# New written orders for every engine, half of the weight transfers on ACT's queue, and a reshaped finish

## The reference: what is computed

```python
for i in range(3):                       # three SSM layers, 64 states
    dbc   = x @ W_dbc[i].T               # delta (1), B (64), C (64)
    delta = softplus(delta @ W_dt[i].T + b_dt[i])
    h_t   = exp(delta * -exp(A_log)) * h_(t-1) + delta * x * B
    x     = (h * C).sum(states) + D * x
    if i < 2: x = mean of neighbouring pairs of steps     # 375 -> 187 -> 93
h = x + attention(layernorm(x))          # 8 heads of 8, Taylor form of softmax
out = h + moe(layernorm(h))              # router, softmax, top 2 of 6 experts, 3-layer MLP each
```

## Time and profile before

| | us |
|---|---|
| median of 3 runs | 836.59 |
| lowest, highest | 832.17, 836.82 |
| the profiled execution: its time | 834.02 |
| the profiled execution: span, first to last instruction | 832.1 |
| PE busy, DVE busy, ACT busy, POOL busy | 708.4, 635.7, 532.2, 330.6 |
| one turn of the steady middle | 44.6 |
| mean granted TensorE clock | 0.953 of full speed |

### The profile page before, as it was taken

One profiled execution on the slowest core, in us unless ns is written; L12 is line 12 of the kernel. 1 busy time (PEld: TensorE's weight loads), 2 busy tenths in 40 slices (PEclk: granted clock), 3 DMA queues, 4 the chain that ended last, 5 costly groups with the idle time before them and its releaser, 6 DMA issues.

```text
span 832.1 us, 18813 instructions
## 1 busy us (share of the span) xinstructions
PE 708.4 (85%) x7751; PEld 318.6 (38%) x7751; DVE 635.7 (76%) x1079; ACT 532.2 (64%) x930; POOL 330.6 (40%) x287
## 2 busy tenths in 40 slices
PE   4665689799989999898989898989989898988773
PEld 2322334244444444443434443444434333433321
DVE  5777869698988888888988888898768895645330
ACT  2334376769686877868686858686766848484630
POOL 4454552325263545354453525263433434121000
PEclk9878899899999999999999999999989999999975
DMA  3223211102021111202030312120110100000001
GB/s 71 55 52 83 47 46 34 33 11 54 19 49 32 45 36 29 52 20 61 8 72 3 69 30 51 31 51 11 44 37 2 34 10 16 15 2 10 7 5 23
DMA packets 78562, 28.30 MB, mean 34 GB/s; under 512 B 70276, under 2 KB 78468, under 8 KB 78468
## 3 DMA queue, kind: packets, MB, share of 16 engines
q1 hardware_dynamic: 75268, 26.43, 14.0%
q10 hardware_dynamic: 3200, 0.58, 0.4%
HBM read 13.28 MB, written 3.05 MB: 20 GB/s over the span
## 4 chain that ended last, share of the span: by engine, by line
PE 57%; DVE 15%; ACT 8%; SPq 7%; DMA 4%; issue 4%; POOL 3%; POOLq 0%; DVEq 0%; ACTq 0%
PE ring L970 16%; PE ring L1038 5%; SPq L554 4%; PE ring L1125 4%; PE ring L1097 4%; PE ring L1026 3%; PE ring L1002 3%; PE ring L1106 3%; PE ring L1062 2%; PE ring L943 2%; PE ring L1088 2%; ACT pm L834 2%; ACT hid L869 2%; PE ring L1054 2%; PE ring L977 1%
## 5 line engine op out<-in xcount | busy, mean ns | idle before, releaser
L834 ACT ACTIVATE pm<-ring,two_col 93x744 f32<-93x744 f32 x128 | 105.2, 871 | 12.8 <-PE ring L1026 11.9
L1402 DVE TENSOR_TENSOR hidw<-hid,ring 128x744 f32<-128x744 f32 x48 | 44.5, 928 | 43.3 <-PE ring L1088 32.4
L690 POOL TENSOR_TENSOR h_in<-base_D,carry_D 128x372 f32<-128x372 f32 x16 | 15.6, 977 | 138.3 <-DVE base_D L1288 112.2
L1038 PE MATMUL ring<-pm,v 97*32 97x93 f32 x2048 | 55.6, 251 | 11.9 <-ACT pm L834 9.0
L770 ACT ACTIVATE soft_A<-ring,bdt_col 128x744 f32<-128x744 f32 x16 | 14.1, 880 | 80.6 <-PE ring L970 80.6
L869 ACT ACTIVATE hid<-ring,b_col 128x372 f32<-128x372 f32 x96 | 49.3, 566 | 23.5 <-PE ring L1106 23.3
L1026 PE MATMUL ring<-q_exp,qk 32*93 32x372 f32 x512 | 57.6, 520 | 7.8 <-POOL q_exp L708 2.6
L1106 PE MATMUL ring<-nrm_f,w 64*64 64x372 f32 x384 | 41.6, 505 | 22.1 <-DVE quad_D L1272 13.0
L686 POOL TENSOR_TENSOR du_C<-delta_C,x_C 128x744 f32<-128x744 f32 x16 | 29.5, 1841 | 75.8 <-ACT delta_C L782 55.6
L693 POOL TENSOR_TENSOR base_C<-base_C,carry_C 128x744 f32<-128x744 f32 x16 | 40.1, 2507 | 48.2 <-DVE base_C L1288 27.0
L1038 PEld LDWEIGHTS ring<-pm,v 97*32 97x32 f32 x2048 | 42.3, 112 | 41.0 <-ACT pm L834 21.7
(11 more groups left out here) (277 smaller groups left out, 1862.2 us busy)
## 6 DMA issues: line engine op xcount, KB each, us to landing
xin_A<-in_x_dram SPq DMA_DIRECT2D x62, 93.0 KB
xin_B<-in_x_dram SPq DMA_DIRECT2D x62, 93.0 KB
x_A<-x_A SPq DMA_DIRECT2D x32, 93.0 KB, 2.2
x_B<-x_B SPq DMA_DIRECT2D x32, 93.0 KB, 2.6
x_C<-x_C SPq DMA_DIRECT2D x32, 93.0 KB, 2.2
out_dram<-osb SPq DMA_DIRECT2D x16, 186.0 KB
x_D<-x_D SPq DMA_DIRECT2D x32, 46.5 KB, 2.0
w<-in_L_ffn_expert_w_dram SPq DMA_DIRECT2D x10, 48.0 KB
```

What stands on the lines that cost most here:

```text
L834: a.activation(pm[q % 2][h][0:TOUT].rearrange("m a j n -> m a (j n)"), out_of(f"att.s{q}{h}")[0:TOUT, :, 0:COLS], ACT.Square, bias=two_col ...
L1038: ins = mm(o[32 * j:32 * j + 32, 0, at:at + TOUT], v1[:, q, H * h + 4 * b + j, :], pm[q % 2][h][:, b, j, :], start=True, stop=True, tile_p ...
L1402: tt(hidw[k][:], hid2[:], out_of(f"ffn.g_{k}")[:, :, 0:COLS], ALU.mult).then_inc(me, 1)
```

## The change

1. All of `ORDER`, `FIRST`, `LAST` and `BANK` are replaced. The steps are the same; their order on each engine, and the banks, are new. The turn is also cut at another place: the new middle starts half a turn earlier in the work, so `FIRST` is shorter and `LAST` longer.
2. 17 of the 36 weight transfers (attention biases and temperature, expert w1, b1, b2) leave SP. ACT issues them, in three new steps of its list: `prep.l2` (7), `prep.l3` (4) and `prep.l5` (6).
3. The flag's matmuls become a PE step `prep.flag` ahead of the last `ffn.h2_2`, its compare a DVE step `prep.again` ahead of the last `ffn.hidw2`. SP reads the flag before it waits for the stores.
4. The last store is cut in two. SP stores sequences 0 to 3, ACT 4 to 7.

```diff
 ORDER = {   # one turn of the middle: before, then after ("..." where cut)
-  "pe": "att.s2:4 D.z:3 A.c:1 ffn.h1_1:5 att.s1:4 C.b:2 B.z:1 C.z:2 ffn.gT:5 A.xT:0 att.y1:4 ...
-         ffn.o:5 att.proj:4 A.dpre:0 C.s:2 C.c:2 att.cen:3 ffn.cen:4 att.var:3 ffn.var:4 B.xT:0 B.c:1 att.qk:3
-         B.dpre:0 att.n2:3 ... A.z:0 A.b:0 ffn.h1_0:4 att.s0:3 A.s:0 ffn.h2_0:4 att.y0:3"
+  "pe": "ffn.g_2:6 A.dpre:1 C.c:3 att.nb1:5 att.nb0:5 att.cen:4 ffn.o:6 att.var:4 att.proj:5 B.c:2
+         ffn.cen:5 att.qk:4 C.s:3 ffn.var:5 att.n2:4 B.xT:1 att.v:4 A.z:1 ffn.h1_0:5 B.dpre:1 ffn.rh:5
+         A.b:1 D.dpre:3 A.s:1 ffn.lg:5 C.dpre:2 B.z:1 att.vs:4 att.s0:4 ffn.h2_0:5 D.z:3 att.y0:4
+         att.s2:4 A.c:1 ffn.h1_1:5 att.s1:4 D.b:3 C.z:2 ffn.gT:5 att.y1:4 ffn.g_0:5 A.xT:0 ffn.h2_1:5 ..."
-  "dve": "... C.base:1 C.based:1 C.carry:1 B.scan:0 att.hn:2 B.carry:0 B.alive:0"
+  "dve": "... ffn.hidw2:5 C.scan:2 att.att1:4 att.att0:4 B.scan:1 C.carry:2 ffn.fin:5 att.mid:4 att.hn:3 B.carry:1
+         ... A.quad:0 att.hat:3 C.alive:2 A.vin:0 A.base:0 ffn.route1:4 D.alive:3 A.scan:0 B.quad:0 ffn.top:4
+         D.quad:2 ffn.gate:4"
-  "pool": "att.qe:4 C.du:2 ffn.split:5 D.du:3 B.du:1 A.y:1 D.y:3 A.pooled:1 C.y:2 B.y:1 C.pooled:2 B.pooled:1 A.du:0"
+  "pool": "B.du:1 C.du:2 A.y:1 D.y:3 A.du:0 B.y:1 C.y:2 C.pooled:2 A.pooled:1 B.pooled:1 att.qe:3 D.du:2 ffn.split:4"
-  "sp": "A.swap:1 D.swap:3 C.swap:2 A.load:0 B.swap:1 ffn.store:7 B.load:0"
+  "sp": "D.swap:3 A.load:0 C.swap:2 B.load:0 ffn.store:7 A.swap:0 B.swap:0"
 FIRST = {
-  "pe": "prep.w0:0 prep.w2:0 A.xT:0 prep.w1:0 A.dpre:0 prep.qkvp:0 B.xT:0 ... A.xT:1 B.c:0 B.xT:1 A.dpre:1 ...
+  "pe": "prep.w0:0 prep.w1:0 A.xT:0 prep.w2:0 A.dpre:0 B.xT:0 ... prep.qkvp:0 A.xT:1 B.s:0 B.b:0 B.c:0 A.dpre:1 A.z:1 B.xT:1 ...
+  "act": "A.x:0 A.exp:0 A.ln:0 B.x:0 A.decay:0 prep.l2:0 B.exp:0 B.ln:0 prep.l3:0 B.decay:0 A.x:1 A.exp:1
+         A.ln:1 A.decay:1 B.x:1 B.exp:1 C.exp:0 C.ln:0 B.ln:1 C.decay:0 A.x:2 B.decay:1 A.exp:2 A.ln:2 prep.l5:0 ...
-  "dve": "... A.alive:2 A.quad:2 prep.late:0 A.vin:2 ...
+  "dve": "... C.base:0 C.based:0 prep.late:0 A.vin:2 A.quad:2 ...
-  "sp": "A.load:0 B.load:0 A.swap:0 prep.l1:0 B.swap:0 A.load:1 B.load:1 prep.l0:0 A.swap:1 B.swap:1
-         prep.l3:0 C.swap:0 A.load:2 prep.l2:0 B.load:2 A.swap:2 prep.l4:0 A.load:3 B.swap:2 D.swap:0 ...
+  "sp": "A.load:0 A.swap:0 A.load:1 B.load:0 B.swap:0 B.load:1 prep.l0:0 A.swap:1 A.load:2 B.swap:1
+         C.swap:0 prep.l1:0 prep.l4:0 A.swap:2 B.load:2 B.swap:2 D.swap:0 A.load:3 C.swap:1 B.load:3 ...
 LAST = {
-  "pe": "... ffn.h1_2:-1 ffn.gT:-1 ffn.g_0:-1 ffn.h2_1:-1 ffn.oT:-2 ffn.g_2:-1 ffn.g_1:-1 ffn.h2_2:-1 ffn.o:-1 ffn.oT:-1"
+  "pe": "... ffn.gT:-1 ffn.g_0:-1 ffn.h2_1:-1 ffn.g_1:-1 ffn.h1_2:-1 ffn.oT:-2 ffn.h2_2:-1 ffn.g_2:-1 ffn.o:-1 ffn.oT:-1"
...
+        MAIN["pe"].insert(MAIN["pe"].index(("ffn.h2_2", NG - 1)), ("prep.flag", NG - 1))
+        MAIN["dve"].insert(MAIN["dve"].index(("ffn.hidw2", NG - 1)), ("prep.again", NG - 1))
+        JOBS["prep.flag"] = (1, "dve prep.again")
+        BANK["prep.flag"] = BANK["ffn.rh"]      # bank 1; ffn.h2_2 now writes banks 0 and 1
...
             walk(MAIN["sp"], do, lambda: None)
-            sp.wait_ge(done["sp ffn.store"], 16 * NG)
             sp.wait_ge(prep["flag"], 1)
             again = sp.value_load(flag_i[0:1, 0:1], min_val=0, max_val=1)
...
+            sp.wait_ge(done["sp ffn.store"], 16 * NG)
+            sp.wait_ge(sem("last_store"), 16)
...
                 if s == "out":
...
+                    if g == NG - 1:
+                        act.wait_ge(me, COUNT["act ffn.out", g])
+                        act.dma_start(out[g * GB + GB // 2:(g + 1) * GB, :, :].rearrange("b t e -> t b e"),
+                                      osb[:, GB // 2:GB]).then_inc(sem("last_store"), 16)
```

More of the change, by code:

```diff
@@ L192, in audio_tower @@
         ORDER = {
[20 rows of a table removed]
[20 rows of a table added]
         }
         FIRST = {
[58 rows of a table removed]
[55 rows of a table added]
         }
         LAST = {
[114 rows of a table removed]
[118 rows of a table added]
         }
         BANK = dict([
-            *((job, 0) for job in "A.c att.s10 A.xT att.s31 ffn.h1_2 ffn.h2_2 D.c ffn.o B.c B.dpre att.v att.vs att.s01 C.gen".split()),
-            *((job, 1) for job in "att.proj att.var".split()),
-            *((job, 2) for job in "att.s21 B.z att.s30 att.nrow att.nb0 A.dpre att.cen att.qk A.z ffn.h1_0 ffn.h2_0".split()),
-            *((job, 3) for job in "att.y3 ffn.oT".split()),
-            *((job, 4) for job in "D.z ffn.h1_1 C.b att.y1 D.b ffn.h2_1 ffn.g_1 D.s B.s C.c B.xT att.n2 C.dpre att.s00 att.y0 A.gen B.gen D.gen prep.w0".split()),
-            *((job, 5) for job in "ffn.gT ffn.lg prep.w1".split()),
-            *((job, 6) for job in "att.s20 att.s11 C.z ffn.g_0 att.y2 B.b ffn.g_2 att.nb1 C.s ffn.cen D.dpre A.b A.s prep.w2".split()),
-            *((job, 7) for job in "ffn.var ffn.rh prep.qkvp".split()),
+            *((job, 0) for job in "A.dpre ffn.o att.n2 A.z A.s att.s01 A.c C.z ffn.h2_1 att.s30 ffn.h2_2 B.gen C.gen D.gen".split()),
+            *((job, 1) for job in "att.cen ffn.rh att.y0".split()),
+            *((job, 2) for job in "att.nb1 att.qk D.dpre C.dpre att.s00 att.s21 att.s11 ffn.g_0 C.b att.s31 B.b prep.w2".split()),
+            *((job, 3) for job in "att.proj att.y3 prep.qkvp".split()),
+            *((job, 4) for job in "C.c ffn.cen B.dpre ffn.lg att.vs ffn.h2_0 att.s20 att.s10 att.y1 ffn.h1_2 B.s D.c A.gen prep.w0".split()),
+            *((job, 5) for job in "ffn.var att.v att.nrow prep.w1".split()),
+            *((job, 6) for job in "ffn.g_2 att.nb0 att.var B.c C.s B.xT ffn.h1_0 A.b B.z D.z ffn.h1_1 D.b ffn.gT A.xT ffn.g_1 att.y2 D.s".split()),
+            *((job, 7) for job in "ffn.oT".split()),
         ])
@@ L464, in audio_tower @@
             for w_, g_ in MAIN[who_] + GENERAL[who_]:
-                if w_[2:] == "gen":
+                if w_[2:] == "gen" or (who_ == "act" and w_[:4] == "prep"):
                     continue
@@ L598, in prepare @@
                          r_b2.rearrange("(a c e) -> a c e", a=1, c=1).broadcast_to([1, 2, NX]), "late")
-                if s == "l2":
-                    load(temp_row[:], temperature.rearrange("a (k h) b c -> (a b c) k h", k=1).broadcast_to([P, 2, H]), "late")
             need = waiter(sp)
@@ L616, in do @@
                     need(g, "act ffn.out")
-                    sp.dma_start(out[bass.ds(g % NG * GB, GB), :, :].rearrange("b t e -> t b e"),
-                                 osb[:]).then_inc(done["sp ffn.store"], 16)
+                    n_out = GB // 2 if g == NG - 1 else GB
+                    sp.dma_start(out[bass.ds(g % NG * GB, n_out), :, :].rearrange("b t e -> t b e"),
+                                 osb[:, 0:n_out]).then_inc(done["sp ffn.store"], 16)
             walk(MAIN["sp"], do, lambda: None)
-            assert n == {"ssm": 8, "qkvp": 2, "late": NLATE}
-            sp.wait_ge(done["sp ffn.store"], 16 * NG)
+            assert n == {"ssm": 8, "qkvp": 2, "late": NLATE - 17}
             sp.wait_ge(prep["flag"], 1)
@@ L886, in experts, with load, prepare @@
                     need(g, "sp ffn.store", back=1)
+                    if g == NG:
+                        act.wait_ge(sem("last_store"), 16)
                     a.activation(osb[:].rearrange("t b e -> t (b e)"), out_of("ffn.oT")[0:TOUT, 0, :],
                                  ACT.Copy).then_inc(me, 1)
+                    if g == NG - 1:
+                        act.wait_ge(me, COUNT["act ffn.out", g])
+                        act.dma_start(out[g * GB + GB // 2:(g + 1) * GB, :, :].rearrange("b t e -> t b e"),
+                                      osb[:, GB // 2:GB]).then_inc(sem("last_store"), 16)
+            def load(dst, src):
+                act.dma_start(dst, src, allow_slow_non_contiguous=True).then_inc(prep["late"], 16)
+            def prepare(g, u, s):
+                for k in range(2):
+                    half = slice(E * k, E * k + E)
+                    if s == "l2":
+                        load(bqk_col[half, :], bqkv[0:P].rearrange("(c e) -> e c", c=2))
+                        load(bv_row[:, k, :], bqkv[P:P + E].rearrange("(a e) -> a e", a=1).broadcast_to([TOUT, E]))
+                        load(bp_col[half, :], bproj.rearrange("(e a) -> e a", a=1))
+                    if s == "l3":
+                        for i in range(2):
+                            load(w1[half, (i ^ k)::2, :], e_w1.rearrange("(c i) d h -> i d c h", i=2)[i])
+                    if s == "l5":
+                        for b in range(2):
+                            load(b1_col[half, b, :], e_b1.rearrange("(c k) h -> k h c", k=2)[k ^ b])
+                        load(b2_col[half, :], e_b2.rearrange("(c k) h -> k h c", k=2)[k])
+                if s == "l2":
+                    load(temp_row[:], temperature.rearrange("a (k h) b c -> (a b c) k h", k=1).broadcast_to([P, 2, H]))
             def do(g, u, s):
```

(21 more changed lines are left out.)

12 lines of the change are left out of this document (1 added, 11 removed), and 385 rows, old and new, of tables (FIRST, LAST, ORDER).

## The result

The changed kernel took 801.6 us (median of 4 runs, 799.94 to 804.88) against 836.7 us of the kernel before in the same comparison: a ratio of 0.960, 95% interval 0.956 to 0.965. I had predicted 814 us and a range of 801 to 835. In a second comparison it took 804.6 us, ratio 0.965 (0.961 to 0.970). The profiled execution took 802.6 us, with a span of 800.9.

A forecast was written before the change was run, and what follows sets the result against it. PE and DVE nearly full in steady turns, transfers pacing the fill; middle 9.1, fill 9, drain 2.6 and finish 2.2 sum to 22.9 off 834.02, giving 811.1, plus 2.6 to the median: 814 us, range 801 to 835.

The forecast's parts named there:

- The block on `top`: Steady turn: POOL's C.du blocks DVE's last `top` instruction 1.47 us; that and PE's 1.72 us wait at `h1_1` go.
- The new waits: Steady turn, PE: about 0.8 us at `y0`, 0.9 at `y1`, 0.3 smaller; 2.0 against 3.3, 1.3 us less per turn.
- The fill: Start of kernel: earlier loads and transfers moved off SP bring steps forward; 9 us gained, bounds 16 to 3 lost.
- My argument that DVE limits the fill: Fill, after `prep.late`: DVE limits, idling 24.8 us between 20 and 120; 9 of 11 to 12 us kept.
- The drain: About four nearly full turns after the middle, half the middle's gain each: 2.6 us, bounds 8 less to 5 more.
- The finish: End of kernel: early flag read and halved store, less a loss on the last path; 2.2 us gained.
- The early reading of the flag: Finish: SP's flag read runs beside the last store; 1.5 us saved, bounds 0 and 4.0.
- The halved store: Finish: two queues feed the last store; 2.0 us saved, bounds 0 and 3.3.
- The loss of 1.3 on the last path: Finish: `h2_2` waits for `prep.again` and `h1_2` moves behind `gT`; 1.3 us lost, bounds 0 and 1.8.
- only fill and finish gain: Rival: in the middle, new waits at `y0` and `y1` cost as much as the old one; 825 us, chance 0.18.
- the queues give nothing: Rival: fill bound by DMA engines, or ACT's steps slip as SP's advance; turns stay the same; 834 us, chance 0.14.
- The slower case: Rival: POOL's `A.du` blocks a DVE scan, 2.8 us in each of 11 turns; 856 us, chance 0.10.

The follow-up runs named there:

- the table of four kernels: Old or new orders, 17 weight transfers on SP or ACT; mixed kernels: new orders with SP 808.15 us, old orders with ACT 833.32 us.
- the kernel with two waits: Changed kernel plus two waits on POOL: B.du of group 4 for D.scan, B.du of group 13 for A.based; 792.17 us, again 792.65.
- six waits: The changed kernel with two POOL waits on B.du, plus four more in the fill on A.du and C.du; 787.67 us, ratio 0.947.

## Why the prediction was right, and where it was not

**The sum.** The kernel came out 12 us faster than the 814 of the forecast, and only 0.6 us inside the range of 801 to 835, a margin smaller than the scatter of the runs. Between the two profiled executions the gain is 31.4 us where 22.9 were forecast: 7.5 more from the middle, 1.6 from the fill, 0.4 from the finish, and 1.3 less from the drain. The rest of the 12 is where the medians lie beside the profiled executions: 2.6 us above before, 1.0 below now.

**The block on `top`.** Right, and shown: taking it out of the kernel before gives 1.09 us per turn. I had counted 1.72 gone and 0.9 to 1.0 of new waits for the whole order.

**The new waits.** This is the mis-sized term of the middle: I expected 2.0 us of PE idle time in a turn, and it was 1.3. At `y0` I expected 0.8 and found 0.57. At `y1` I expected 0.9 and found none; 0.35 stands at the scores, on ACT's squares too. I had counted the work between `s1` and `y1` by itself, as if PE came to `s1` without a wait, and had put ACT's two `hid1_1` instructions behind it. In the rows they start at 408.03, 0.16 us ahead of `s1`, so the squares are done at 410.77, just before `y1` (410.83). My reading of the timeline, which no experiment tests, is that a delay on ACT is paid once, not again at each wait in its path. Further, PE's busy time fell by 0.4 us per turn, which I had taken as fixed at 41.3 and as the floor of a turn in any order; why the same instructions take less was not tested. Together that is 2.4 against the 1.3 of the forecast: over seven turns 16.6 us against 9.1.

**The fill.** 9 us was forecast and 10.6 measured, but by other steps than mine. `A.x:1` came at 32.4 as forecast (32.5) and `A.exp:1` at 36.1 (34.5). The third A load was issued at 37.0 (36), but transposed only at 50.2, where I said 45, and `quad_A` of group 2 came at 69.5, where I said 59. `prep.late` started at 64.0, not 58, and not for the reason that I gave: it did not wait for ACT's six transfers. DVE came to that wait at 63.10 and passed it at once, and works there without a gap:

```profile
63.09 0.99 DVE L1315 SCALAR_TENSOR_TENSOR base_C<-x_C,d_col,base_C 128x744 f32<-128x744 f32 x1
64.00 0.28 DVE L1267 TENSOR_TENSOR blk_cen<-ident,blk_mean 128x128 f32<-128x128 f32 x1
```

The step that failed is DVE's own work ahead of `prep.late`, which I put at nothing. Its own instructions take another 4.7 us, to 68.7, where I gave them 1. The fourth B transpose came at 96.6, not 90. The gain appeared only behind that: `quad_B` of group 2 was 15 us earlier (72.0 against 87.2) and `quad_A` of group 3 12 us (99.2 against 111.6). I had read the steps singly; the table of four kernels shows that orders and queue work only together. My argument that DVE limits the fill fits: it is busy 88 of 100 us, and with four blocks of 5.7 us taken from it the steady turns start 5.4 to 7.2 us earlier. The steps failed and the sum stood partly by luck.

**The drain.** 2.6 us forecast, 1.3 measured, with the stall at 536 us in it; in the repeated profile of the changed kernel it is 0.8 us lost. Without the stall the drain won 4.1 and 6.8 us in the two profiles of the kernel with two waits, so the stall of 5.1 us is the term that I had left out. The long issue of SP behind a store, costed at nothing, did cost nothing: `A.swap` behind it took 1.17 us.

**The finish.** 2.2 us forecast, 2.6 measured, again from wrong parts. The early reading of the flag is worth 3.1 in the profiles and not 1.5. The halved store is worth nothing or half a microsecond less, where I took 2.0; the Trainium skill ("DMA: Bandwidth & Descriptors", section "Issuing engines are not separate DMA queues") spoke against it and was right: a wait of 6.5 us with two queues, 6.0 with one. The loss of 1.3 on the last path is there in part, but hidden. From the start of `gateT` to that of `fin` it took 13.6 us before and after. Up to `o`, though, it took 10.4 us instead of 9.6, and `o`'s twelve matmuls took 3.14 us instead of 3.99, with a granted clock of 0.66 over that stretch instead of 0.50. That the two cancel is luck.

**The rivals.** That only fill and finish gain (825 us) and that the queues give nothing (834) are refuted by the turns and by 107.53 against 101.24. One half of the second did show in the old orders, where ACT's issues pushed its own steps back by 2.9 us and the other queue gave nothing. The slower case was right in its mechanism and wrong in who loses: DVE's scan starts about 0.05 us ahead and POOL waits. In the kernel as it is this order holds in all seven turns. The rule of the Trainium skill that the first to issue keeps the port ("SBUF — State Buffer", section "Who interferes with whom") fits both sides of it, by the numbers above. The trace goes further than the rule: a DVE instruction that lost once kept waiting through a whole run of POOL instructions. What I missed is the same contention outside the steady turn, where it cost 10 us in two places and 5 to 7 more in four.

## What to carry to other kernels

Look in the timeline of DVE for instructions that are longer than their twins, and see what POOL runs beside them; a single wait on POOL, which has idle time, can give a bounding DVE its time back. Do this for the ends as well as for the steady turn: here six waits outside it gave 17 us by the medians, and undoing the block in every turn of the kernel before gave 9. And before moving transfers to another queue, see whether the first queue was late at all: a gap that they filled is not won.
